# Where the low halves of weights and tiles are subtracted: GpSimd or VectorE, in a cross-attention and expert kernel

## The reference

```python
lat = layer_norm(layernorm(x)) ; ctx = layer_norm(ctx_1024)       # both over 256 columns
q = lat @ Wq ; k, v = split(ctx @ Wkv) ; k = rope(k, cos, sin)
attn = softmax(clip(q k^T / 8, -11, 11)) ; x = x + (attn v) @ Wo + bo
y = layernorm(x)
sel = sigmoid(y @ expert_sel^T) ; scores = relu(y @ keys[e])
x = x + sum_e sel[e] * (scores[e] @ values[e])
```

## Time and profile before

| | us |
|---|---|
| median of three runs (all: 1019.45, 1013.47, 1018.41) | 1018.41 |
| the profiled execution, whole time | 1021.36 |
| its span, from the first to the last instruction | 1019.6 |
| pairs 0 to 31, from the first exponential to the last | 29.4 to about 816 |
| mean granted TensorE clock (share of full speed) | 0.997 |

### The profile page before, as it was taken

How to read it: one execution, slowest core, us unless ns; L and a number is a source line. 1 busy time by engine, 2 the same in 40 slices (tenths; PEclk the granted TensorE clock), 3 DMA queues, 4 the chain that set the end, 5 groups by cost and what they waited for, 6 DMA issues and landing times. The chain is left out here.

```text
span 1019.6 us, 16015 instructions
## 1 busy us (share of the span) xinstructions
PE 982.0 (96%) x5712; PEld 622.8 (61%) x5712; DVE 816.5 (80%) x1235; ACT 532.0 (52%) x765; POOL 210.0 (21%) x172
## 2 busy tenths in 40 slices
PE   4989999999999999999999999999999899999998
PEld 3645555555555555555555555555555368888898
DVE  7788999999898989998988887987889776545322
ACT  3656656666666656565556655554555532222221
POOL 3222312112011121111111000320000035445443
PEclk9999999999999999999999999999999999999999
DMA  7343323332322322232333223222222481332321
GB/s 216 109 131 94 110 84 109 99 94 69 104 75 89 89 73 89 77 102 88 93 84 95 63 84 84 83 83 84 85 63 64 125 269 52 126 124 85 113 108 49
DMA packets 68570, 99.84 MB, mean 98 GB/s; under 512 B 21840, under 2 KB 44624, under 8 KB 66448
## 3 DMA queue, kind: packets, MB, share of 16 engines
q1 hardware_dynamic: 68496, 98.89, 32.0%
HBM read 70.01 MB, written 10.75 MB: 79 GB/s over the span
## 5 line engine op out<-in xcount | busy, mean ns | idle before, releaser
L1125 ACT ACTIVATE wide_a<-score_ps 128x1024 f32<-128x1024 f32 x256 | 248.9, 1026 | 116.6 <-PE score_ps L885 116.4
L1419 DVE TENSOR_SCALAR wide_a<-wide_a 128x1024 f32<-128x1024 f32 x256 | 181.0, 734 | 49.2 <-ACT wide_a L1125 48.6
L1428 DVE TENSOR_TENSOR p_sum<-wide_a 128x1024 f32<-128x1024 f32 x128 | 161.2, 1259 | 2.3
L898 PE MATMUL o_ps<-wide_a,values_a 128*64 128x512 f32 x512 | 124.2, 605 | 3.2 <-DVE wide_a L1419 1.9
L898 PE MATMUL o_ps<-wide_a,v_sb 128*64 128x512 f32 x512 | 124.1, 605 | 1.4 <-issue 1.4
L885 PE MATMUL score_ps<-q_hi,k_hi 64*128 64x512 f32 x512 | 115.0, 446 | 3.9 <-ACT wide_a L1125 2.2
L885 PEld LDWEIGHTS score_ps<-q_hi,k_hi 64*128 64x128 f32 x512 | 47.8, 183 | 114.2 <-issue 75.6
L1929 DVE SCALAR_TENSOR_TENSOR act<-h_ps,wide_a 128x512 f32<-128x512 f32 x64 | 44.2, 690 | 89.1 <-PE h_ps L150 83.8
L1855 ACT CAST act_hi<-act 128x512 fp32r<-128x512 f32 x64 | 39.8, 621 | 138.1 <-DVE act L1929 138.1
L1729 POOL TENSOR_TENSOR act_lo<-act,act_hi 128x512 fp32r<-128x512 f32 x64 | 84.7, 1324 | 95.9 <-ACT act_hi L1855 95.9
L885 PE MATMUL score_ps<-q_hi,k_lo 64*128 64x512 f32 x512 | 101.3, 392 | 0.0
(11 more groups left out here) (220 smaller groups left out, 1970.1 us busy)
## 6 DMA issues: line engine op xcount, KB each, us to landing
wide_a<-sel_dram SPq DMA_DIRECT2D x16, 1024.0 KB, 4.8
k_swap<-k SPq DMA_DIRECT2D x124, 128.0 KB, 2.3
w_hi<-packs_hi SPq DMA_DIRECT2D x26, 384.0 KB, 3.0
w_lo<-packs_lo SPq DMA_DIRECT2D x26, 384.0 KB, 3.6
den<-inv_dram SPq DMA_DIRECT2D x64, 128.0 KB, 2.9
ctx_raw<-ctx SPq DMA_DIRECT2D x24, 128.0 KB, 2.2
packs_hi<-w_hi SPq DMA_DIRECT2D x8, 384.0 KB, 3.3
packs_lo<-w_lo SPq DMA_DIRECT2D x8, 384.0 KB, 3.9
```

What stands on the lines that cost most here:

```text
L898: mm = pe.matmul(o_ps[DH * h:DH * h + DH, :], v_sb[n // 2 % 2][:, at:at + DH], probs[s % RING][:, h, :], start=(s == 0), stop=(s == STEPS ...
L1125: act.activation(probs[s % RING][:], score_ps[s % 2][:], ACT.Exp, scale=DH ** -0.5).then_inc(exp_done, 1)
L1419: dve.tensor_scalar(probs[s % RING][:], probs[s % RING][:], CLIP_HI, CLIP_LO, ALU.min, ALU.max).then_inc(clipped, 1)
L1428: dve.tensor_tensor(p_sum[m][:], first, second, ALU.add).then_inc(summed_up, 1)
```

## The change

`split_tile` is now VectorE's. `split_weights` and `split_v_weights`, which VectorE already had for the first weights, are now used for all of them, and GpSimd's own three functions are gone. In VectorE's program `split_weights(n+2)` stands in m = 2 after the first sum of four, in pairs 0 to 5; `split_tile(n+10)` stands at the end of m = 3 in pairs 0 to 21, and `split_v_weights` behind it in pairs 0 and 2. GpSimd keeps the roots, the first tiles, and the head and keys at the end of the phase. Semaphores and their counts are the same.

```diff
@@ gpsimd
-            def split_tile(t):
-                pool.wait_ge(tile_hi, blocks(t + 1))
-                pool.tensor_tensor(ctx_at(ctxT_lo, t), ctx_t32[:], ctx_at(ctxT_hi, t),
-                                   ALU.subtract).then_inc(tile_split, 1)
-                if has_x(t):
-                    pool.tensor_tensor(x_at(xT_lo, t), x_t32[:], x_at(xT_hi, t), ALU.subtract).then_inc(tile_split, 1)
-            def split_weights(w):
-                par = w % 2
-                pool.wait_ge(w_hi_done, 2 * (w + 1))
-                pool.tensor_tensor(w_lo[par][:], w_raw[:, 0:WC], w_hi[par][:], ALU.subtract).then_inc(w_split, 1)
-            def split_v_weights(j):
-                par = j % 2
-                pool.wait_ge(wv_hi_done, j + 1)
-                pool.tensor_tensor(wv_lo[par][:], wv_raw[:], wv_hi[par][:], ALU.subtract).then_inc(wv_split, 1)
@@ gpsimd, iteration(n)
                 if t < TILES:
                     rstd(t)
-                if n + 2 < PAIRS:
-                    split_weights(n + 2)
                 if n == 0:
                     split_first(4)
-                if t < TILES:
-                    split_tile(t)
-                if n % 2 == 0 and n // 2 + 2 < DUOS:
-                    split_v_weights(n // 2 + 2)
@@ vector
+            def split_tile(t):
+                dve.wait_ge(tile_hi, blocks(t + 1))
+                dve.tensor_tensor(ctx_at(ctxT_lo, t), ctx_t32[:], ctx_at(ctxT_hi, t),
+                                  ALU.subtract).then_inc(tile_split, 1)
+                if has_x(t):
+                    dve.tensor_tensor(x_at(xT_lo, t), x_t32[:], x_at(xT_hi, t), ALU.subtract).then_inc(tile_split, 1)
@@ vector, iteration(n)
                         if not last:
                             sum_quad(n, 0)
+                        if n + 2 < PAIRS:
+                            split_weights(n + 2)
                         if n == 29:
                             invert_gate(dve, sh, 0, 1)
                     if m == 3:
+                        if t < TILES:
+                            split_tile(t)
+                        if n % 2 == 0 and n // 2 + 2 < DUOS:
+                            split_v_weights(n // 2 + 2)
                         if n == 23:
                             split_sel()
```

## The result

| | before | after |
|---|---|---|
| median, us | 1018.73 (20 runs, 1013.47 to 1021.12) | 1013.55 (20 runs, 1009.91 to 1017.66) |
| ratio | | 0.9954, 95% interval 0.9942 to 0.9966 |
| span of the profiled execution | 1019.6 | 1011.3 |
| pairs 0 to 6 in it, first exponential to first exponential | 183.2 | 178.2 |

The account below looks back on a forecast made before the run. TensorE, busy 96%, was taken to set the time wherever it does not pause; 2.6 + 1.7 + 3.0 + 0.1 - 0.3 = 7.1 us off the median 1018.41 gave 1011.3, range 1005.5 to 1017.

Parts of the forecast that it names:

- Long clips are GpSimd's doing: VectorE, first pairs: clips up to 2.33 us against a median of 0.69 wait out GpSimd's subtractions beside them.
- Pair 0, 2.6 us: Pair 0: `rope_add` and ScalarE's work behind it move up, so pair 1's scores start 2.6 us earlier.
- The clock, 1.7 us: TensorE in pair 1: pause shrinks from 2.19 to 1.5 us, no fall to half clock expected, 1.7 us gained.
- the clock doesn't come back: Rival, chance 0.18: a 1.5 us pause and the earlier 0.7 us ones suffice for the fall; 1013.0 us.
- Pairs 3 to 6, 3.0 us: Start of pairs 3 to 6: TensorE's losses 1.93, 0.64, 1.01, 0.63 become about 0.8, 0.2, 0, 0.2; 3.0 us gained.
- Pairs 1 and 2, 0.1 us gained: Pairs 1 and 2: a gain of 0.1 us at most.
- the relief turns into waits for transfers: Rival, chance 0.16: spread or k swap waits; pairs 3 to 6 gain nothing, 1014.1 us, or 1016 with late swaps.
- Pair 18, 0.3 lost: Pairs 17 to 18: `scale_o` waits for the spread, so nothing comes back and the tile costs 0.3 us.
- The queues: SyncE's later weight loads and weights' readiness cost nothing; up to 0.8 us lost in pairs 0 and 2 if swap delayed.

Follow-up runs that it names:

- load-alone kernel: Kernel before plus VectorE subtractions of the same sizes and places on its own data, GpSimd keeping its remainders: 1029.62 us, ratio 1.0105.
- tiles alone: Against the kernel before, only the tiles' remainders moved to VectorE; weights and value weights stay on GpSimd: 1017.70 us, ratio 0.9987.
- relief alone: Kernel after with each moved remainder cut to two columns, so neither engine has the work: 1010.39 us, ratio 0.9923 to the kernel before.
- third profile of the kernel after: Kernel after, unchanged, run again beside the stored-twice kernels: 1013.88 us, ratio 0.9936 to the kernel before.
- the reorder: Kernel after with VectorE's weights' remainder moved between `split_k` and `scale_o`: 1011.59 us (0.9934), built again 1010.72 us (0.9910).
- the doubled store: Kernel after with pair 1's store of inverse denominators done twice and the weights' remainder moved before `scale_o`: 1013.01 us, ratio 0.9933.
- stored twice: Kernel after with pair 1's store of inverse denominators done twice before the spread, VectorE's order unchanged: 1015.07 us, ratio 0.9952.

## Why the prediction was right, and where it was not

**Long clips are GpSimd's doing: right.** The load-alone kernel keeps them, and so does the one that leaves the weights there (eight clips over 1.5 us in each); every kernel that takes the weights off GpSimd loses them (one or two over 1.5 us, all of them behind 640 us). VectorE's busy total fell by 7.0 us (7 forecast), GpSimd's by 63.9 (65).

**Pair 0, 2.6 us: right.** 2.3 us in the profiled execution, 2.3 and 2.7 in the two other profiles of the kernel after (28.94 and 28.55 us). The pause at its end is 1.83, not 1.5, because TensorE gained 2.2 us (counted from the clip on) instead of 1.9 in front of it; that changes no sum.

**The clock, 1.7 us: the step that failed.** The fall near 60 is gone in the profile after, as forecast. But the kernels with the load alone and with the tiles alone keep a pause of 2.19 us at that place, and ran pair 1 at full clock:

```profile
60.40:84.90 24.50, 23.82 (x140) 13.22 (x138) 23.38 (x33) 15.60 (x24) 8.32 (x6) 1.00 0.45 135
```

```profile
60.50:84.90 24.40, 23.72 (x140) 13.18 (x138) 22.07 (x33) 15.73 (x24) 4.14 (x3) 1.00 0.49 143
```

So the pause does not bring the fall of the earlier trace rows every time. The other executions point the same way: mean granted clock 0.9969 and 0.9962 over 13 and 29 of the kernel before, 0.9966 and 0.9974 over 20 and 8 of the kernel after, where a fall that costs 1.7 us, in every execution of the one and in none of the other, would make a difference of 0.0017. These means count falls anywhere in the kernel, so how often pair 1 has one stays open. The step read a rule (a pause of 2.19 us, then the fall) out of two cases in one trace, and booked a chance event as a gain. The rival "the clock doesn't come back", 1013.0, gave the time that came, by luck; its reason, that shorter pauses are enough for a fall, has some support too: in the third profile of the kernel after the clock fell in pair 2 behind the pause of 1.88 us. That the profiled executions differ by 8.3 us and the medians by 5.2 is mostly this and pair 27, where the first of them fell to half clock and the second didn't:

```profile
697.00:725.30 28.30, 26.11 (x142) 15.04 (x140) 22.27 (x27) 14.35 (x19) 2.42 (x1) 0.94 0.20 57
```

```profile
692.00:718.70 26.70, 24.54 (x142) 13.87 (x140) 22.29 (x26) 14.31 (x19) 2.39 (x1) 1.00 0.21 60
```

There too it is no gain of the change: two of its three profiles show the fall (pair 27 is 29.15 and 28.7 us long in them).

**Pairs 3 to 6, 3.0 us: right.** 3.2 us by their lengths, 3.1 by TensorE's idle time, with 0.85, 0.18, 0 and 0.12 left, where 0.8, 0.2, 0 and 0.2 was forecast. The relief alone brings them to 96.8 us, with no idle time in them, so the load takes 1.4 of it back. The sum by the rows held: six of the long clips of the kernel before lie in pairs 0 to 5, one beside each of the weights' remainders, and each took 2.3 us, 1.6 more than usual. The Trainium skill ("SBUF — State Buffer", section "Who interferes with whom") has the later instruction wait for the other's whole time; by that rule, and the 2.08 us of the earlier trace rows, the upper bound was 2.1. The trace agrees: in pair 0 the clip began with 1.75 us of GpSimd's instruction to go, and gave back 1.63.

**Pairs 1 and 2, 0.1 us gained: wrong, a loss of 1.5.** The step said of the weights: TensorE needs them 1.2 us into the pair, they are ready 0.3 to 0.5 us before it begins, "both cost nothing". There was a margin in the pairs whose spread comes in time: in pair 0 the weights were ready at 58.07 and wanted at 58.98, in pair 2 at 108.98 and 110.75. The step left out that the remainder now stands behind a wait for a DMA, whose own lateness was in the rows: the earlier trace rows show one of 1.42 us. In pair 1 `scale_o` waits 1.5 to 2.1 us for the spread in the three profiles, and the pause is 1.3 to 1.9, so that only 0.2 to 0.6 us of margin was there. The forecast had "the relief turns into waits for transfers" as a rival, and named the spread, but priced it in pairs 3 to 6, where nothing of it came, and not in what is queued behind it.

**Pair 18, 0.3 lost: wrong.** It takes 24.4 us with no idle time, 0.2 less. What was read as a place where the spread comes last in every execution was a store that took 2.4 us once; in the profile after it takes 1.4.

**The queues: half right.** "Up to 0.8 us is lost" if the value weights push the swap of k back: VectorE waited 2.96, 1.88 and 3.60 us for `k_swap` in pair 1 in the three profiles after, and not at all before. In the first and third `q_lo` then came late for TensorE, and pair 1 took 24.95 and 25.55 us instead of the 24.4 to 24.5 of the second and of every other profile in which the clock stayed up there: 0.5 and 1.1 lost, 0.5 in the mean. TensorE in the third:

```profile
76.41 0.41 PE L767 MATMUL job_ps<-ident,ctx_n 128*128 128x128 f32 x2 [0.83 <-DVE q_lo L1356]
```

It was priced, and left out of the sum.

So 2.6 + 3.0 came, 1.7 was not there to come, and 1.5 + 0.5 were lost that were not in the sum. Pairs 0 to 6, less 1.7 us for each fall of the clock, are 3.3, 4.4 and 3.0 us shorter in the three profiles after than in the one before, 3.6 in the mean, where 5.7 was forecast. The medians differ by 4.0 and 5.2. The rest of 0.4 to 1.6 us stays open: it is less than what pair 27 alone varies between executions (26.7 to 30.2 us in the fourteen profiles). Both errors point the same way, 3.7 us of gain too many; the time came only 2.2 us above the forecast because of this rest, and that much of it is luck.

## What to carry to other kernels

Two engines that slow each other down can make an offloaded instruction cost more than it saves (here about 1.6 us lost for 0.87 saved): ask what the busy engine's own instructions take beside it, before calling the offload free. When work is moved into an engine's program, look at the last wait ahead of its new place, and put it in front of that wait if its inputs are there; a margin that is reckoned without that wait is none. Never book a gain for an event that the one profiled execution shows once or twice, as a clock fall or a late transfer, without asking how often it comes.

## What the runs showed of the hardware

**A small transfer was late where a packet of instructions fell on it.** In all fourteen profiles a 16 KB packet of the instruction queue began 0.7 to 2.7 us after the issue of the store in pair 1. In seven of them (0.70 to 1.34 us after) the 4 KB store took 2.8 to 3.4 us, in the seven others (1.08 to 2.72 us after) 1.4. In each of the seven a single part of 16 was late. Where both ranges overlap, something else decides, perhaps which of the 16 DMA engines carries the packet. Nor is it a matter of chance alone: the seven are all the profiles of kernels in which VectorE has the weights' remainder (or its two columns) behind `scale_o`, and the seven others are those in which it stands before `scale_o` or on GpSimd. Why the order of VectorE's program should set this stays open. It means that the reorder may also win by making the store punctual; the doubled store shows that the pause is gone even where the spread is late.

**The length of a pause does not tell whether the clock falls.** Three windows of TensorE behind pauses of 1.88 (kernel after, third profile), 3.05 (stored twice) and 3.90 us (load alone), the granted clock third from last:

```profile
86.90:90.40 3.50, 3.50 (x10) 2.41 (x8) 3.43 (x7) 0.58 (x1) 0.00 (x0) 0.54 0.83 264
```

```profile
87.00:91.00 4.00, 3.92 (x18) 2.57 (x20) 3.96 (x7) 1.18 (x2) 0.00 (x0) 1.00 0.59 181
```

```profile
120.50:127.30 6.80, 6.29 (x24) 2.56 (x26) 5.02 (x10) 3.03 (x4) 1.07 (x1) 0.50 0.04 10
```

The shortest had the fall to 1.2 GHz, for 3.4 us; the middle one, at almost the same place in the program, none; the longest had one of 6.8 us. In pair 27 of the fourteen profiles the pause is 2.17 to 4.26 us long: the clock fell in none of the three with 2.17, and in nine of the eleven with 2.19 or more. So a longer pause makes a fall likelier, without deciding it.
